# a1 normalised on VectorE inside the pseudo-inverse, with a one-column multiply on GpSimd and round zero released by bank

## The reference

```
q, k, v = split(xn @ w_qkv)              # 8 heads of 16
q_l, k_l = means of q and k over blocks  # 16 landmarks
a1 = softmax(q @ k_l^T)                  # tokens x landmarks
a2 = softmax(q_l @ k_l^T)                # 16 x 16
a3 = softmax(q_l @ k^T)                  # landmarks x tokens
z = a2^T / (max column sum * max row sum)
for _ in range(6):                       # pseudo-inverse
    xz = a2 @ z
    z = 0.25 * z @ (13 I - xz @ (15 I - xz @ (7 I - xz)))
out = a1 @ z @ (a3 @ v) + conv33(v)      # residual: 33 taps along the tokens
x = x + out @ w_out + b_out
```

## Time and profile before

| | us |
|---|---|
| median of three runs | 355.32 (354.33 to 356.91) |
| time of the profiled execution | 352.09 |
| its span, first to last instruction | 350.3 |
| TensorE matmul busy | 295.9 (84%) |
| VectorE busy | 196.1 (56%) |
| ScalarE busy | 158.8 (45%) |
| GpSimd busy | 39.1 (11%) |

### The profile page before, as it was taken

One profiled execution on the slowest core, in us unless ns is written; L12 is line 12 of the kernel. 1 busy time (PEld: TensorE's weight loads), 2 busy tenths in 40 slices (PEclk: granted clock), 3 DMA queues, 4 the chain that ended last, 5 costly groups with the idle time before them and its releaser, 6 DMA issues.

```text
span 350.3 us, 6471 instructions
## 1 busy us (share of the span) xinstructions
PE 295.9 (84%) x1952; PEld 193.5 (55%) x1952; DVE 196.1 (56%) x460; ACT 158.8 (45%) x341; POOL 39.1 (11%) x37
## 2 busy tenths in 40 slices
PE   8999999999885888988999778977867877777872
PEld 3665777775432467987997346666622453225510
DVE  4686998864177665788766533411331493226620
ACT  1097677774361356354561241111024285445930
POOL 5200090001000050005200000242000000000001
PEclk9999999999998999999999996999895899989988
DMA  3954200000000000000000222231000000000000
GB/s 86 242 97 102 67 0 2 2 2 2 0 0 0 1 2 0 2 0 1 0 2 0 46 59 59 63 58 44 0 1 6 17 0 0 17 17 0 0 0 30
DMA packets 9108, 8.98 MB, mean 26 GB/s; under 512 B 3932, under 2 KB 8668, under 8 KB 8796
## 3 DMA queue, kind: packets, MB, share of 16 engines
q1 hardware_dynamic: 8820, 8.39, 10.7%
q10 hardware_dynamic: 264, 0.30, 0.3%
HBM read 8.42 MB, written 0.26 MB: 25 GB/s over the span
## 4 chain that ended last, share of the span: by engine, by line
PE 61%; DVE 15%; ACT 9%; issue 7%; DMA 3%; DVEq 1%; SPq 1%; POOL 1%; POOLq 0%
PE ps L581 10%; PE ps L524 6%; PE ps L589 5%; PE ps L744 3%; DMA recA<-rec_a 3%; PE ps L750 3%; PE ps L543 2%; PE ps L879 2%; PE ps L732 2%; ACT arena L1218 2%; DVE rmax L1664 2%; PE ps L992 2%; PE ps L871 1%; ACT arena L1052 1%; PE ps L610 1%
## 5 line engine op out<-in xcount | busy, mean ns | idle before, releaser
L1338 DVE TENSOR_TENSOR arena<-arena 128x512 f32 x72 | 44.4, 689 | 7.8 <-ACT arena L1052 4.5
L524 PE MATMUL ps<-xC,cstb 128*128 128x512 f32 x94 | 47.6, 651 | 0.0
L1059 ACT ACTIVATE arena<-ps 128x512 f32<-128x512 f32 x72 | 37.7, 602 | 15.7 <-PE ps L581 15.6
L581 PE MATMUL ps<-cstb,arena 128*128 128x128 f32 x288 | 36.3, 277 | 0.7 <-DVE arena L1338 0.7
L581 PEld LDWEIGHTS ps<-cstb,arena 128*128 128x128 f32 x288 | 31.0, 140 | 9.4 <-DVE arena L1338 8.6
L524 PEld LDWEIGHTS ps<-xC,cstb 128*128 128x128 f32 x94 | 19.0, 213 | 25.8 <-issue 25.6
L589 PE MATMUL ps<-arena 128*32 128x256 f32 x288 | 19.2, 385 | 0.0
L744 PE MATMUL ps<-arena 128*128 128x160 f32 x96 | 15.3, 307 | 2.7 <-DVE arena L1522 1.5
L1218 ACT ACTIVATE arena<-ps,rmax 128x256 f32<-128x256 f32 x32 | 14.9, 471 | 5.2 <-DVE rmax L1664 5.2
L1237 ACT ACTIVATE arena<-ps,w2c 128x512 f32<-128x512 f32 x16 | 9.7, 688 | 15.6 <-PE ps L992 15.6
L744 PEld LDWEIGHTS ps<-arena 128*128 128x128 f32 x96 | 13.3, 190 | 3.8 <-DVE arena L1522 2.4
(11 more groups left out here) (371 smaller groups left out, 540.4 us busy)
## 6 DMA issues: line engine op xcount, KB each, us to landing
arena<-rec_a SPq DMA_DIRECT2D x19, 128.5 KB
toepb<-toep SPq DMA_DIRECT2D x1, 1536.0 KB
w32b<-w SPq DMA_DIRECT2D x1, 1225.0 KB
cstb<-cst SPq DMA_DIRECT2D x1, 1044.0 KB
recA<-rec_a SPq DMA_DIRECT2D x3, 128.5 KB
arena<-rec_b SPq DMA_DIRECT2D x19, 16.5 KB
w1b<-moe_w SPq DMA_DIRECT2D x1, 264.0 KB
xC<-x SPq DMA_DIRECT2D x1, 256.0 KB, 2.8
```

What stands on the lines that cost most here:

```text
L524: mm(ps[7], ident if lhs is None else lhs, xC if rhs is None else rhs, start=True, stop=True)
L581: last = tr(ps[c % BI][:, (q * PT + t) * P:(q * PT + t + 1) * P], ST[:, c, t, q * 8:q * 8 + 8, :], ident)
L1059: af(SQ[:, c].rearrange("p q n -> p (q n)"), ps[c % BI], ACT.Copy).then_inc(S["s_ev"], 1)
L1338: tt_(ST[:, c], hy.unsqueeze(3).to_broadcast([P, PT, 16, 16]), hx.unsqueeze(2).to_broadcast([P, PT, 16, 16]), ALU.mult).then_inc(S["prod"], 1)
```

## The change

On GpSimd the four multiplies of a1 go away, and a multiply of one column of a tile of zeros stands behind the partition maximum; nobody waits for it. On VectorE the sums of the last block of a1 (`a1_sums(BI - 1)`) move from ahead of round 0 to between its two halves; a wait for all sums stands ahead of the loop; and each round 1 to 4 multiplies one block of a1, 128x512, between its two halves, at an address taken from the loop's register. On TensorE round 0 no longer waits for all four residual banks: each pair waits for its own.

```diff
--- before.py
+++ after.py
@@ -466,6 +466,7 @@
             pool.wait_ge(S["cr_in"], 1)
             nc.gpsimd.partition_all_reduce(small[:, 32:34], small[:, 16:18], P, bass.bass_isa.ReduceOp.max
                                            ).then_inc(S["cr_max"], 1)
+            nc.gpsimd.tensor_tensor(zeros[:, 0:1], zeros[:, 1:2], zeros[:, 2:3], ALU.mult)
 
             def stage_residual(bi):
                 r4 = res.rearrange("p (t b n) -> p b t n", t=PT, b=BI)
@@ -477,11 +478,6 @@
             pool.wait_ge(S["res_ev"], 4)
             stage_residual(0)
 
-            for bi in range(BI):
-                pool.wait_ge(S["a1_sum"], bi + 1)
-                v = arr3(a1[:, 512 * bi:512 * bi + 512], 16)
-                nc.gpsimd.tensor_tensor(v, v, small[:, 256 + 32 * bi:288 + 32 * bi].unsqueeze(2)
-                                        .to_broadcast([P, 32, 16]), ALU.mult).then_inc(S["a1_norm"], 1)
             for bi in range(1, BI):
                 pool.wait_ge(S["res_mm"], BI + bi)
                 stage_residual(bi)
@@ -736,8 +732,9 @@
 
             pe.wait_ge(S["z0_set"], 1)
 
-            def pinv_step(it, meanwhile):
+            def pinv_step(it, meanwhile, bank_free=lambda q: None):
                 for q in range(4):
+                    bank_free(q)
                     pe.wait_ge(S["y_bd"], it * 4 + 3 + q)
                     for j in range(2):
                         b = 2 * q + j
@@ -770,8 +767,7 @@
                                   ident)
                     last.then_inc(S["a1T_mm"], 1)
 
-            pe.wait_ge(S["res_ev"], 4)
-            pinv_step(0, nothing)
+            pinv_step(0, nothing, lambda q: pe.wait_ge(S["res_ev"], q + 1))
             pe.wait_ge(S["a1_sub"], BI)
             with pe.Fori(1, PINV - 1) as it:
                 pinv_step(it, turn_residual)
@@ -1502,9 +1498,15 @@
                     m.unsqueeze(2).to_broadcast([P, 32, 16]), ALU.subtract).then_inc(S["a1_sub"], 1)
                 if bi:
                     a1_sums(bi - 1)
-            a1_sums(BI - 1)
-
-            def pinv_step(it, dst, lo):
+
+            def a1_normalise(it):
+                v = arr3(a1.rearrange("p (b n) -> p b n", b=BI)[:, bass.ds(it - 1, 1), :]
+                         .rearrange("p b n -> p (b n)"), 16)
+                r = small[:, 256:384].rearrange("p (b n) -> p b n", b=BI)[:, bass.ds(it - 1, 1), :]
+                tt_(v, v, r.rearrange("p b n -> p (b n)").unsqueeze(2).to_broadcast([P, 32, 16]), ALU.mult
+                    ).then_inc(S["a1_norm"], 1)
+
+            def pinv_step(it, dst, lo, between):
                 for q in range(4):
                     b2 = slice(2 * q, 2 * q + 2)
                     yv = ps[q][:, 0:320].rearrange("p (b c) -> p b c", b=2)[:, :, P:P + 32]
@@ -1512,6 +1514,7 @@
                     stt(pG[:, b2], Yz[:, b2], 7.0, yv, ALU.mult, ALU.subtract)
                     dve.wait_ge(S["lin_set"], it * 4 + 1 + q)
                     stt(pR[:, b2], yv, -3.75, pH[:, b2], ALU.mult, ALU.add).then_inc(S["rest_set"], 1)
+                between(it)
                 for q in range(4):
                     b2 = slice(2 * q, 2 * q + 2)
                     wy = ps[q][:, 320:512].rearrange("p (b c) -> p b c", b=2)[:, :, 0:32]
@@ -1524,11 +1527,12 @@
                         ).then_inc(S["y_bd"], 1)
 
             dve.wait_ge(S["z0_set"], 1)
-            pinv_step(0, bdY, 0)
+            pinv_step(0, bdY, 0, lambda it: a1_sums(BI - 1))
+            dve.wait_ge(S["a1_sum"], BI)
             own.restart()
             with dve.Fori(1, PINV - 1) as it:
-                pinv_step(it, bdY, 0)
-            pinv_step(PINV - 1, bdZ.rearrange("p b h m -> p b (h m)"), 16)
+                pinv_step(it, bdY, 0, a1_normalise)
+            pinv_step(PINV - 1, bdZ.rearrange("p b h m -> p b (h m)"), 16, lambda it: None)
             dve.wait_ge(S["w2_mm"], 1)
             v_.tensor_copy(w2_bd[:, 4:8], ps[1].rearrange("p (b h e) -> p b h e", b=4, h=HEADS)
                            ).then_inc(S["w2_evD"], 1)
```

## The result

The changed kernel took **0.9886** of the time of the kernel before, 95% interval 0.9847 to 0.9924, where of each kernel only the executions within some 1.5% of its fastest one are compared. Over all executions the two medians are nearly the same, 355.2 us (348.4 to 365.0, 20 runs) against 355.3 us (351.9 to 367.0, 20 runs), so a gain is seen in the faster executions only. The profiled execution of the changed kernel has a span of 346.6 us against 350.3, 3.7 us less.

What follows compares the result with a forecast made beforehand. TensorE's chain bounds the kernel, with 2.74 us lost in rounds 1 and 2 to VectorE standing behind GpSimd; -2.74 - 0.15 + 0.1 = -2.8 us takes the median 355.32 to 352.5 us, range 350.4 to 355.3.

Steps and rivals of the forecast that it cites:

- The four multiplies taken from GpSimd: Rounds 1 and 2: without GpSimd's a1 multiplies VectorE's four masked copies return from 1106 to 425 ns, -2.74 us.
- The four multiplies on VectorE: Rounds 1 to 4: one multiply each in VectorE's idle time, within TensorE's slack of 0.50 to 0.61 us; cost 0.
- the cover: TensorE's slack in rounds 1 to 4 that hides VectorE's new multiply; without it the cost would be 2.4 us.
- The staging copies: Rounds 1 to 3: GpSimd's residual copies meet VectorE's new multiply; nothing to 0.3 us over three rounds, taken as 0.1.
- the two orders that I allowed for: After the multiply: GpSimd and VectorE alternate, first masked copy 0.15 us later; or both copies first, last pair 0.1 late.
- Round 0 by bank: TensorE starts round 0 1.19 us earlier, but VectorE's sums now stand there; taken as -0.15 us, bounds 0 and -1.19.
- Rival C: Round 0 pays in full: VectorE fits the sums in a pause, TensorE keeps its 1.19 us; 351.5 us, chance 0.12.
- The one-column multiply: GpSimd behind the partition maximum: pays the 7.33 us start-up at 141.3, ends near 148.6, before the first copy; cost 0.
- What follows shifts with it: Behind the pseudo-inverse: one dependent chain that shifts with it, so the -2.8 us carry to the whole time.
- Rival A: One-column multiply does not pay the start-up; it falls on the first linear-attention layer, +6.0 us; 358.5 us, chance 0.07.
- Rival B: VectorE bounds rounds 1 to 4, the multiply waiting for GpSimd's copies or starting late; 353.3 to 354.5 us, chance 0.15.
- The Trainium skill's rule on two SBUF inputs: A VectorE instruction with two SBUF inputs and a GpSimd instruction reading SBUF exclude each other for the whole instruction; sum unchanged.

Runs made afterwards that it cites:

- the move alone: Kernel before with the four a1 multiplies moved to VectorE and the one-column multiply; round 0 and sums as before: stretch 41.24 us against 43.91, ratio 0.9871.
- the version with the sums first: Changed kernel with the sums of the last a1 block ahead of round 0 again: pseudo-inverse stretch 40.28 us against 40.95, ratios 0.9909 and 0.9917.
- the doubled multiply: Changed kernel with one more a1 multiply, into an unused block, in each of rounds 1 to 4: pseudo-inverse stretch 43.25 us, 2.29 more than the changed kernel.

## Why the prediction was right, step by step

**The four multiplies taken from GpSimd: -2.74.** Right, and 0.09 too large. The masked copies are at 426 ns in all rounds, and the move alone gave -2.67 for this and the next two terms together. The prediction set 9.70 us for two undisturbed rounds; with the move alone rounds 1 and 2 take 9.79, since the first L741 of the loop keeps the 2.31 us that the earlier trace rows show. That this and the 0.1 for the copies cancel is luck.

**The four multiplies on VectorE: 0.** Right, and with the margin I gave: L1523 follows at 0.60 us behind the multiply's start, TensorE waits nowhere in rounds 2 to 5. "If the cover were gone it would cost 4 x 0.61 = 2.4 us" was not tested. That the doubled multiply cost 2.29 is near it by chance, as its rounds of 5.48 us lost 0.27 by waiting and 0.36 by longer products.

**The staging copies: +0.1.** Their size was right (1.31 us for two, pushed behind the multiply), their cost is 0 in TensorE's chain. The first masked copy kept its 0.42 us, and GpSimd's second copy was the one that waited, so neither of the two orders that I allowed for came.

**Round 0 by bank: -0.15.** Right in kind: the sums on VectorE ate most of the 1.19 us. It is -0.28 measured: round 1 starts 0.55 us earlier and its L741 takes 0.28 longer than the 2.31 before. My L1520 at 156.74 came at 156.55, since ScalarE's four evacuations ran without a gap from 154.03 to 155.22 and did not wait for TensorE. Rival C, that VectorE fits the sums in, is what the version with the sums first does: -0.96. I had put "1.02 us at one piece" against it; the 1.13 us that VectorE idles ahead of its first combination hold just that.

**The one-column multiply: 0.** Its mechanism was right: it pays 7.42 us at 141.3. But I missed that it also is a way to the gain of its own: without it the four multiplies met the masked copies because of the 7.33 us pause, and with it alone 1.82 us are saved.

**What follows shifts with it.** This was the weak step. The chain of waits behind round 5 is the same and the layers take 25.4 us in both profiles, but with the clock behind the pseudo-inverse the span moved by +0.99 and -1.76 us, that is 0.8 of the 3.7. Over many executions the time is spread over 17 us, with the median of the changed kernel between 352.8 and 356.5 from one group of runs to the next. The prediction warned of the clock in its last sentence and gave it a scatter of 1 us. The ratio 0.9886 makes 1.1% of gain, 4.1 us [2.7, 5.4], where I had 2.8, which the interval holds. The stretch shows 2.95 of it; the rest is not traced to the change. And the 352.5 us that I gave for the median did not come: over all executions it is 355.2, 0.1 below the kernel before. The 2.8 us are right for the pseudo-inverse, and for the whole time only where the clock is alike.

**Rival A** had its place right (the first L488, 5.4 us of waiting where 6.0 were worked out) and its price wrong: +3.2 us forecast against the kernel before; measured are 21 by the ratio and 17 between the medians of executions on one chip. The term that was left out is the clock, at half speed for the 44 us from 225.5 on. By my figure the one-column multiply guarded against 6 us; in the profile the layers took 18.2 more without it.

**Rival B** did not occur; its mechanism was seen only with two multiplies.

The Trainium skill's rule on two SBUF inputs, page "SBUF — State Buffer", section "Who interferes with whom", agrees with the runs in its main part: VectorE's two masked copies that met GpSimd's multiplies took 0.66 and 1.03 us, and GpSimd's copies that met the new multiply 1.31 for two. Its part that a loser is blocked for the whole instruction fits both: they end 0.28 us behind the ends of two multiplies, whatever was left of these.

## What to carry to other kernels

When two engines share a way to memory, ask when their instructions meet rather than how many there are: one line that moved a start-up pause was worth 1.82 of 2.95 us. Slack on an engine is free up to its edge and can cost more than the excess beyond it. A wait of TensorE of a few microseconds ahead of a stretch with short products and gaps is to be priced with the clock that may be lost over the whole stretch, here 12.7 us on top of 5.4. And where the whole time scatters by 17 us, a gain of 3 us is read from its own stretch, at like clock.

## What the runs showed of the hardware

- The first TENSOR_TENSOR on GpSimd after the partition maximum pays a pause that no instruction shows: 7.33 us ahead of a 128x512 multiply, 6.64 to 7.55 ahead of a one-column one in eleven profiles, 7.0 more idle time ahead of a 128x1024 one. Copies between the maximum and the multiply did not pay it (they start 0.06 us behind their release), nor did the TENSOR_TENSORs ahead of the maximum (L460 and L462 run at 125.06 and 127.39 with at most 0.08 us between).
- A VectorE TENSOR_TENSOR of 128x256 with both inputs in SBUF that meets a GpSimd multiply ends 0.28 to 0.29 us behind the end of that multiply: six of six, 0.66 to 1.34 us long instead of 0.43.
- TensorE's clock fell to half in the linear-attention layers and stayed there for 37.5 and 37.6 us in two profiles of one kernel and for 44.4 us in a third, of the version without the one-column multiply, where it fell during a wait; in the first TensorE was busy 31.3 of the 37 us that cover the layers. With small products in the gaps it stayed at full there in both profiles, and 24 executions had a mean of 0.935 or more.
- The spread of mean granted clock between executions of one unaltered kernel is 0.899 to 0.958, and its times 348.3 to 365.0 us.
